# Macaron layer with two mixtures of experts: weights streamed past 128 stationary tokens in float32, each FFN in two turns of tokens

## The reference, cut to what matters

```python
# x: 16 batches x 256 tokens x 128; 8 experts, top 2, hidden 256; 16 heads of 4
x = x + 0.5 * ffn(layernorm(x), ...)
x = x + attention(layernorm(x), ...)          # softmax attention on the left 64 columns
x = x + 0.5 * ffn(layernorm(x), ...)          # the same weights again

def ffn(x, gate_w, gate_b, w0, b0, w1, b1, w2, b2):
    xt = x.reshape(-1, 128)                   # 4096 tokens
    logits = xt @ gate_w.T + gate_b           # 8 a token
    top_v, top_i = top_k(logits, 2)
    h0, h1 = xt @ w0[e].T + b0[e], xt @ w1[e].T + b1[e]     # 256 wide, for each expert e
    act = h0 * silu(h1)
    out = act @ w2[e].T + b2[e]               # 128 wide
    return softmax(top_v) . out[top_i]        # the two experts' rows, weighted
```

## Time and profile before

| | us |
|---|---|
| three runs | 880.24, 880.10, 875.22 |
| median | 880.1 |
| the profiled execution's own time | 880.13 |
| its span in the trace | 878.4 |
| mean granted TensorE clock | 0.876 of full speed |
| busy in the span: TensorE, VectorE, ScalarE, GpSimd | 539.3, 582.1, 393.3, 483.7 |

### The profile page before, as it was taken

The page is one execution under the profiler, slowest core; times in us unless marked ns, Lnnn a source line. Parts: engine busy times, 40 slices in busy tenths (PEclk is TensorE's granted clock), DMA queues, the critical chain, the costliest instruction groups (busy, mean ns, idle before and its releaser), DMA issues. The chain is left out here.

```text
span 878.4 us, 15667 instructions
## 1 busy us (share of the span) xinstructions
PE 539.3 (61%) x4422; PEld 406.5 (46%) x4422; DVE 582.1 (66%) x1878; ACT 393.3 (45%) x863; POOL 483.7 (55%) x584
## 2 busy tenths in 40 slices
PE   1222213999931468888877788778841296977830
PEld 1121213999930125555545455444420285867720
DVE  2346461888852677888878788878332196979928
ACT  1011012888820016666555555556620285757710
POOL 1367775566637974554656564422344256877850
PEclk9999999999975559999989899999975598998965
DMA  7211122333311211211112111110000222222226
GB/s 253 74 42 41 37 72 80 87 104 105 99 58 37 60 52 46 59 56 53 58 41 65 42 62 45 51 42 15 15 30 32 74 67 62 72 77 67 72 86 240
DMA packets 48705, 59.92 MB, mean 68 GB/s; under 512 B 10908, under 2 KB 40668, under 8 KB 47804
## 3 DMA queue, kind: packets, MB, share of 16 engines
q1 hardware_dynamic: 39420, 40.81, 15.2%
q0 software_dynamic: 8640, 17.84, 6.3%
q10 hardware_dynamic: 560, 0.27, 0.1%
HBM read 30.96 MB, written 27.44 MB: 66 GB/s over the span
## 5 line engine op out<-in xcount | busy, mean ns | idle before, releaser
L1074 DVE TENSOR_REDUCE attn_nm<-ps 128x2 f32<-128x512 f32 x256 | 170.1, 685 | 58.1 <-PE ps L777 41.7
L884 ACT ACTIVATE attn_pt<-ps 128x512 f32<-128x512 f32 x256 | 147.5, 597 | 105.7 <-PE ps L761 78.6
L299 POOL DMA_INDIRECT x_rows<-route_xn,route_rows x128 | 129.9, 1015 | 74.9 <-DVE route_rows L288 39.0
L777 PE MATMUL ps<-attn_ka,attn_qa 128*128 128x256 bf16 x512 | 109.7, 302 | 58.5 <-DVE attn_nm L1074 28.7
L761 PE MATMUL ps<-attn_qa,attn_ka 128*128 128x256 bf16 x512 | 103.0, 286 | 23.1 <-ACT attn_pt L884 12.2
L621 POOL DMA_INDIRECT y_tokens<-experts_y_tokens,experts_to x78 | 77.5, 993 | 54.1 <-DVE experts_y_tokens L540 35.9
L437 PE MATMUL ps<-experts_x_hi,experts_w 128*128 128x256 f32 x312 | 96.8, 310 | 7.0 <-issue 7.0
L438 PE MATMUL ps<-experts_x_lo,experts_w 128*128 128x256 f32 x312 | 89.9, 288 | 0.0
L439 PE MATMUL ps<-experts_x_hi,experts_w 128*128 128x256 f32 x312 | 89.9, 288 | 0.0
L777 PEld LDWEIGHTS ps<-attn_ka,attn_qa 128*128 128x128 bf16 x512 | 41.2, 103 | 94.7 <-DVE attn_nm L1074 48.2
L583 POOL CAST experts_w<-w_table 128x1536 fp32r x39 | 59.0, 1514 | 40.2 <-ACT experts_y L494 40.2
(11 more groups left out here) (178 smaller groups left out, 1286.3 us busy)
## 6 DMA issues: line engine op xcount, KB each, us to landing
experts_x<-x_rows SPq DMA_DIRECT2D x78, 130.0 KB
y_rows<-experts_y_tokens SPq DMA_DIRECT2D x39, 128.0 KB, 1.7
second_y<-y_tokens SPq DMA_DIRECT2D x16, 256.0 KB, 4.8
kq_pieces<-attn_kqp SPq DMA_DIRECT2D x16, 192.0 KB
x_rows<-no_rows SPq DMA_DIRECT2D x16, 130.0 KB
x_rows<-route_xn,route_rows POOLq DMA_INDIRECT x128
out<-x_tokens SPq DMA_DIRECT2D x16, 128.0 KB, 1.8
x_tokens<-x SPq DMA_DIRECT2D x7, 256.0 KB, 6.6
```

Source lines behind the costliest of these rows:

```text
L299: nc.gpsimd.indirect_dma_start(out=x_rows[:, :], out_offset=to, in_=xn[:, g % RX, t, :], in_offset=None).then_inc(sent[g % RX], 16)
L777: mm = pe.matmul(ps[:, SA[k], j * S:(j + 1) * S], qa[sl][:, h, qc * P:(qc + 1) * P], ka[sl][:, h, :], start=True, stop=True)
L884: nc.scalar.activation(pt[:, g % 2, j, :], ps[:, SBK[h % 2], :], ACT.Exp, scale=SCALE).then_inc(exp_done, 1)
L1074: nc.vector.tensor_reduce(nm[:, qc, 2 * pair:2 * pair + 2], ps[:, SA[k], :].rearrange("p (j t) -> p j t", t=S), AX.X, ALU.max, negate=True ...
```

## The change

- Each FFN has two turns of 2048 tokens (4 groups). A turn has its own list of at most 40 blocks of 128 slots, taken as 20 pairs; 40 pairs an FFN. There are two tensors `x_rows`, used in turn.
- In the first FFN only groups 0 to 3 are routed ahead of the blocks. Groups 4 to 7 are routed beside the 20 pairs of the first turn, at steps written out in TOP; their list is made at step 13. The list of the second FFN's first turn is made inside attention. The routing of the last group moves from the end of attention to the first steps of the second FFN's blocks, and the list of the last turn with it.
- The zeroing of `kq_pieces` moves behind the first loads of x; VectorE doesn't wait for it any more.
- The tokens are stationary and the weights move. `w_table` and `w2_table` hold plain float32; no split, no copies of weights. TensorE reads 10 experts at a time into registers and takes the weights at a register address. First layer: one float32 matmul of 512 columns for each half of the pair (w1 and w0 side by side). Second: two of 128 columns, after four transposes of the activation a pair.
- The biases are added by a bf16 matmul: `b_table` has each expert's biases as three bf16 pieces, on 24 partitions; `chosen` has, for each expert, ones on its three rows.
- For one pair ScalarE has silu and the copy of the transposed activation (512 elements each), VectorE the product (512), the copies of x and y (256 each), and in the second FFN three small operations in `dve_to`.
- SP reads 8 tail rows and 10 start rows at a time, and loads x by two DMAs a pair. A tail is 128 rows.
- In the second FFN, the y rows of the first 8 batches are loaded, added and stored beside the pairs of the last turn, from its fourth pair on.

```diff
+TURNS = 4
+TURN_GROUPS = 2 * GROUPS // TURNS
+SLOTS = 128
+PAIRS = -(-((2 * TURN_TOKENS + E * (SLOTS - 1)) // SLOTS) // 2)
+LISTED = 2 * PAIRS
...
+        w_table = sb("w_table", [P, E, WCOLS])
+        w2_table = sb("w2_table", [P, E, HID])
+        b_table, chosen = sb("b_table", [P, BCOLS], BF16), sb("chosen", [P, E, P], BF16)
...
+    def starts_of(eng, turn, blocks):
+
+        cols = listed[0:1, turn, 0, blocks.start:blocks.stop]
+        return nc.values_load_multi_w_load_instructions(cols, engines=(eng.engine,), min_val=0, max_val=ROWS - SLOTS)[1]
...
+    def streamed(table, e, at, n):
+        return table[:, bass.ds(e, 1), at:at + n].rearrange("p a w -> p (a w)")
...
+    def pe_first(pe, q):
+        pe.wait_ge(xT_done, q + 1)
+        wait(pe, act_done, q - 1)
+        if q % PAIRS % AT_ONCE == 0:
+            turn, js = some(q)
+            pe.wait_ge(route["list_ready"], 3 * (turn + 1))
+            for j, e in zip(js, route["experts_of"](pe, turn, js)):
+                expert[turn * LISTED + j] = e
+        for i in range(2):
+            e, o = expert[2 * q + i], ps[:, q % 2 * 2 + i, :]
+            pe.matmul(o, m["xT"][:, q % 2, i], streamed(w_table, e, W1, 2 * HID), start=True, stop=False)
+            mm = pe.matmul(o, streamed(chosen, e, 0, P), b_table[:, 0:2 * HID], start=False, stop=True)
+        mm.then_inc(h_ready, 1)
+
+    def pe_turn(pe, q):
+        pe.wait_ge(act_done, q + 1)
+        wait(pe, at_done, q)
+        for i in range(2):
             for k in range(CH):
...
+                mm = pe.transpose(ps[:, AT, (i * CH + k) * P:(i * CH + k + 1) * P], m["act"][:, q % 2, i, k * P:(k + 1) * P],
+                                  const["ident"][:])
+        mm.then_inc(aT_ready, 1)
+
+    def pe_second(pe, q):
+        pe.wait_ge(at_done, q + 1)
+        wait(pe, y_copied, q)
+        for i in range(2):
+            e, o = expert[2 * q + i], ps[:, Y, i * P:(i + 1) * P]
+            for k in range(CH):
+                pe.matmul(o, m["actT"][:, q % 2, i, k], streamed(w2_table, e, k * P, P), start=(k == 0), stop=False)
+            mm = pe.matmul(o, streamed(chosen, e, 0, P), b_table[:, 2 * HID:BCOLS], start=False, stop=True)
         mm.then_inc(y_ready, 1)
...
+    def pe(pe, q, own):
+        if q in own:
+            pe_first(pe, q)
+        if q + AHEAD in own:
+            pe_x(pe, q + AHEAD)
+        if q - TURN_LAG in own:
+            pe_turn(pe, q - TURN_LAG)
+        if q - Y_LAG in own:
+            pe_second(pe, q - Y_LAG)
...
+        for at in route["tails_of"](sp, turn):
+            sp.dma_start(x_rows[turn % 2][bass.ds(at, SLOTS), :], const["no_rows"][:, 0]).then_inc(tails, 16)
         sp.wait_ge(route["list_ready"], 3 * (turn + 1))
         route["all_sent"](sp, turn)
...
+    def sp_x(sp, q):
+        turn = q // PAIRS
+        if q % PAIRS == 0:
+            sp_list(sp, turn)
+        if q % PAIRS % AT_ONCE == 0:
+            _, js = some(q)
+            for j, at in zip(js, route["starts_of"](sp, turn, js)):
+                start[turn * LISTED + j] = at
...
+    TOP = {4: 1, 5: 4, 6: 8, 7: 11}
+    FIND = (2, 15)
+    LIST = TOP[7] + 2
...
-            dve.wait_ge(zeros_out, 16 * NB)
...
             route["dve_norm"](dve, 1)
-            for g in range(GROUPS):
+            for g in range(TURN_GROUPS):
...
+                if g == 0:
+                    dve.wait_ge(upto_done, 2)
+                    nc.vector.tensor_reduce(taken[:], const["piece"].rearrange("p (e i) -> p e i", i=PIECES), AX.X,
+                                            ALU.add).then_inc(chosen_made, 1)
+                    dve.wait_ge(chosen_made, 2)
+                    nc.vector.tensor_copy(chosen[:], taken[:].unsqueeze(2).broadcast_to([P, E, P])).then_inc(chosen_made, 1)
+                if g == 1:
+                    dve_biases(dve)
...
+            for q in all_steps:
+                blocks["sp"](sp, q, own)
+                if q == own.start:
+                    for b in range(NB):
...
+    HALF_OUT, TAKE = 4, 6
...
+                if q == middle + HALF_OUT:
+                    blocks["out_to"](sp, middle)
+                    sp_load(sp, range(NB // 2))
+                if 0 <= q - middle - TAKE - 1 < NB // 2:
+                    sp_store(sp, q - middle - TAKE - 1)
```

More of the change, by code:

```diff
@@ L190, in pe_transpose @@
         pe.wait_ge(xn_ready, g + 1)
-        wait(pe, prod_done, g - len(BANKS[g // GROUPS]) + 1)
+        for before in [i for i in range(g) if bank(i) == bank(g)][-1:]:
+            pe.wait_ge(prod_done, before + 1)
+            turn, at = divmod(before, TURN_GROUPS)
+            if at == TURN_GROUPS - 1:
+                pe.wait_ge(list_ready, 3 * turn + 1)
+                pe.wait_ge(list_step, LIST_STEPS * turn + 1)
         for t in range(TG):
@@ new lines, in y_offset, with experts_of @@
+    def y_offset(tile, r):
+        g, t = divmod(tile, TG)
+        return bass.IndirectOffsetOnAxis(ap=y_at[:, g, r, t:t + 1], axis=0)
+    def starts_of(eng, turn, blocks):
+        cols = listed[0:1, turn, 0, blocks.start:blocks.stop]
+        return nc.values_load_multi_w_load_instructions(cols, engines=(eng.engine,), min_val=0, max_val=ROWS - SLOTS)[1]
+    def experts_of(eng, turn, blocks):
+        cols = listed[0:1, turn, 1, blocks.start:blocks.stop]
+        return nc.values_load_multi_w_load_instructions(cols, engines=(eng.engine,), min_val=0, max_val=E - 1)[1]
@@ L374, in sem, with experts @@
+def experts(nc, c, route, const, tables, ps, x_rows, y_rows, y_tokens):
+    XR, YR, IR = 4, 4, 6
+    AT_ONCE = 5
+    XT, AT, Y = 4, 5, 6
+    AHEAD, TURN_LAG, Y_LAG = 2, 1, 2
+    ONE = PAIRS * (TURNS // 2)
+    w_table, w2_table, b_table, chosen = tables
     def sem(n):
@@ L402, in allocate @@
         sb("y_tokens", [P, YR, 2, P])
-        if turn:
+        if ffn:
+            sb("first", [P, 2, 2])
             sb("row", [P, 2, 2])
             m["to"] = late.enter_context(nc.sbuf_tensor("experts1_to", [P, IR, 2], U32))
-    def steps(turn, before, after):
-        own = range(turn * LISTED, (turn + 1) * LISTED)
-        return range(own.start - before, own.stop + after), own
-    def wait_out(eng, j):
-        first = len(range(j % YR, LISTED, YR))
-        uses = j // YR + 1
-        wait(eng, y_out[j % YR], 16 * min(uses, first))
-        wait(eng, y_sent[j % YR], 32 * (uses - first))
@@ L419, in pe_x, with steps, wait_out, some @@
-    def pe_x(pe, j):
-        pe.wait_ge(x_in[j % XR], 16 * (j // XR + 1))
-        wait(pe, xlo_done, j)
+    def steps(ffn):
+        own = range(ffn * ONE, (ffn + 1) * ONE)
+        return range(own.start - AHEAD, own.stop + Y_LAG + 1), own
+    def wait_out(eng, q):
+        first = len(range(q % YR, ONE, YR))
+        uses = q // YR + 1
+        wait(eng, y_out[q % YR], 16 * min(uses, first))
+        wait(eng, y_sent[q % YR], 32 * (uses - first))
+    def some(q):
+        turn, at = divmod(q, PAIRS)
+        return turn, range(2 * at, min(2 * (at + AT_ONCE), LISTED))
@@ new lines, in sp_y, with sp @@
+    def sp_y(sp, q):
+        sp.wait_ge(y_copied, q + 1)
+        sp.dma_start(y_rows[q * 2 * SLOTS:(q + 1) * 2 * SLOTS, :].rearrange("(i p) d -> p i d", i=2),
+                     m["y_tokens"][:, q % YR]).then_inc(y_out[q % YR], 16)
+    def sp(sp, q, own):
+        if q == own.start - AHEAD:
+            for i in range(XR):
+                sp_x(sp, own.start + i)
+        n = q + AHEAD + XR - 1
+        if n in own and n >= own.start + XR:
+            sp_x(sp, n)
+        if q - Y_LAG - 1 in own and q - Y_LAG - 1 < ONE:
+            sp_y(sp, q - Y_LAG - 1)
@@ L1571, in _ @@
+            blocks["out_to"](sp, own.stop)
+            sp_load(sp, range(NB // 2, NB))
+            for b in range(NB // 2, NB):
+                sp_store(sp, b)
             sp.wait_ge(stored, 16 * NB)
```

735 lines of the change are left out of this document (338 added, 397 removed).

## The result

The changed kernel takes 963.25 us (median of 4 runs, 961.48 to 965.88); the kernel before, run beside it, 880.17: ratio 1.096, interval 1.090 to 1.101. The forecast was 883 us, the range 850 to 928. The profiled execution has a span of 959.9 us at a mean clock of 0.872.

What follows compares the result with a forecast made beforehand. The prediction saw no single bound before, and TensorE's 3.9 us pairs bounding both FFNs' blocks after; +15.7 (first FFN), +1 (attention) and -13.5 (second FFN) gave +3.2 on 878.4, forecast 883 us, range 850 to 928.

Steps and rivals of the forecast that it cites:

- The pair: TensorE's work for two blocks of 128 slots: 3.9 us, with the other engines' work all under that.
- R3: Rival: on TensorE a float32 column costs one cycle an instruction, 68 us less, about 815 us; chance 0.07.
- The start: Routing of half the tokens ahead of the first FFN: first block at 91 us, where it was 147.06.
- I take 2 us hidden, 1.3 exposed: 7 batches after the first, 9.1 us an FFN: TensorE's register reading of ten experts every 5 pairs: 3.3 us a batch, partly covered by its queue.
- R1: Rival: TensorE's register batches exposed nearly in full, and addresses costing issue time: +41 us, 924 us; chance 0.26.
- half clock in the blocks: TensorE's clock at half in the FFN blocks, named among what would make all the theories wrong.
- The rest of the first FFN: First FFN's blocks besides the batches: pairs 156 us, routing 6.2, half-clock start 1.7, tables and waits 3, drain 1.2.
- The start of the second FFN: SP's chain from the last group's routing start to the first block: 21.5 us, where it was 46.4.
- The slack of 2 us at the second turn: First FFN: the second turn's x arrives at step 17.4, needed by step 18; each us beyond is on the path.
- R4: Rival: routing doesn't fit beside the first FFN's blocks, +22 us, 905 us; sign: gap at the 21st pair; chance 0.03.
- Attention's +1: Attention keeps its work and gains one list of blocks made inside it: 1 us longer.

Runs made afterwards that it cites:

- e7: e1's kernel with the first layer's operands rounded to float32r and multiplied in one instruction instead of two, less exact: 808.26 us, ratio 0.956.
- e10: e1's kernel run again, on the same chip as e9: 857.91 us, ratio 1.013.
- e6: Changed kernel with the eight tails of the second FFN's first turn written by SP at the end of attention: 908.84 us, ratio 1.072.
- e4: Changed kernel with the last turn's eight tails written by SP at its step 6 in the second FFN: 961.04 us, ratio 1.083.
- e5: Changed kernel with all of attention's block list but the two operations reading the counts moved two groups later: 913.34 us, ratio 1.078.
- e9: The changed kernel itself, run again on another chip: 914.17 us, ratio 1.080.
- e3: Changed kernel with the same batches of ten read one pair earlier, right behind the first layer's matmuls: 939.12 us, ratio 1.062.
- e2: Changed kernel with the batches of ten numbers that TensorE reads placed 64 bytes apart: 946.89 us, ratio 1.071.
- e1: Changed kernel with TensorE reading two experts ahead of each pair instead of ten ahead of every fifth: 916.37 us, ratio 1.035.
- e8: Changed kernel with the edits of e1, e4, e5 and e6, attention's last sends moved behind it, y loaded in twos: 838.51 us, ratio 0.990.
- e12: e8's edits with e7's one-pass float32r first layer, less exact there: 791.71 us, ratio 0.935.

## Why the prediction was wrong, by its own steps

| from the trace, us | forecast | measured |
|---|---|---|
| first block matmul | 91 | 86.1 |
| first FFN's blocks | 177.2 | 200.4 |
| attention, to the last update of x | 399.0 | 404.5 |
| to the second FFN's first block | 22.0 | 31.8 |
| its blocks | 171.7 | 214.5 |
| tail | 20.8 | 22.7 |
| span | 881.6 | 959.9 |

- **The pair was right**: 3.9 forecast, 3.92 measured, and one that needs nothing else on the way: no other engine's work is in it. That a float32 column costs two instructions of two cycles, read from attention's 379 against 277 ns, held (e7: half the instructions, 1.22 us less). R3 falls.
- **The start was right** to 5 us, on the early side: the last send before it began at 71.2 (73.5 forecast), and the eight tails took 4.0 us to issue where 11 were taken.
- **The step that failed is "I take 2 us hidden, 1.3 exposed: 7 batches after the first, 9.1 us an FFN".** The mechanism was named, and R1 was its full price, but the batch was mis-sized. The load: 1.5 taken, 1.1 or 2.5 measured, 1.84 in the middle. The arithmetic: 1.75 taken by its recorded length, 2.9 by its pitch. Hidden: 2 taken, 2.4 measured at the sixth reading, but 0.9 at the second, behind a few short matmuls of the routing. The gaps are 21.3 and 19.1 us where 9.1 each were forecast. The Trainium skill (Runtime: NRT & Kernel Launch, section Instruction fetch mechanics), as quoted with the sum, has about 200 ns a register, stated there for loads from HBM. By it ten registers would take 2.0 us, an estimate; the trace, whose numbers lie in SBUF, has 1.1 and 2.5.
- **What no step had is the clock behind the gaps.** The forecast gave 1.7 us an FFN to it, for a cold start, and named half clock in the blocks only as what would make all wrong. The windows have 0.96 and 0.89 of full clock in the blocks. With it, the reading costs 56 us (e10), where the forecast had 18 (14 x 1.3) and R1 51 (14 x 3.65). R1, with 0.26 of the chance and 924 us, comes closest, in part by luck: its 3.65 a batch is above the mean gap of 2.9, and the clock, which it did not have, makes up for that.
- **The rest of the first FFN was right.** Without readings the forecast for its blocks is 168.1 us (177.2 - 9.1); e10, which hides them, has 168.5 (82.86 to 251.32). For the second FFN it is 162.6 against 180.4, where x comes late twice in e10 (6.90 and 3.14).
- **The start of the second FFN missed 10 us**, the beginning of its code, for which VectorE waits 8.5 us. The forecast started SP at the statistics as if nothing stood between. The chain from SP's first reading, at 699.8, to the first block was 22.9 us where 21.5 were forecast, which is near by luck: the tails took 4.0 and not 8.5, and the readings, the landing and TensorE's own batch more than they were given. e6 takes 9.1 of it away.
- **The slack of 2 us at the second turn** was worked out for the first FFN alone, where it held: no gap at its 21st pair. In the second FFN x of a pair waits also for VectorE's places of the pair four before (`dve_to`), so SP starts its list one pair later: 6.98 us (e4). That is R4's sign, a gap at the 21st pair, but in the other FFN. The loads of y and the reading of ten starts behind them (869.7 to 877.1 in SP's queue) hold up x once more: 2.57.
- **Attention's +1** was 6.5. The list holds VectorE 3.4 us at a stretch (573.0 to 576.5 in the changed kernel), and by e5 a batch is 3.7 us longer for it. Why the rest, e5 doesn't say.

So of the 78 us missed, some 38 are the reading and its clock (56 less the 18 forecast), 10 the change of code, about 10 late x, 5 attention; the start is 5 better, the tail 2 worse. The remaining some 18 go with the 'remote' waits in the blocks, which end in a gap of 5.15 us on TensorE at 750.86, and their half clock: on e9's chip, almost without them, the change costs 66 us instead of 83. That last part is argued from two profiles, not shown by an experiment.

## What to carry to other kernels

A register reading on the bounding engine is priced by its pitch in the queue, not by the lengths of its rows; keep each one shorter than what the engine's queue covers (here two values each pair instead of ten each fifth), and, as e3 has it, put it behind the longest instructions. A gap on TensorE is paid twice when the clock falls behind it: sum the gaps, then look at the durations of the matmuls behind each. Streaming float32 at 4 cycles a column is paid for in full wherever TensorE is the bound: here 1.2 us of 3.9 a pair, which only the earlier start and shorter tail can earn back, and then by 1%.

## What the runs showed of the hardware

- A load of ten 4-byte values into TensorE's registers took 1.07 to 1.27 us for the first and third batch of a turn and 2.4 to 2.6 for the second and fourth, where the batches lie 40 bytes apart; on SP's queue, from the same tile, 0.95 to 1.3 and 2.1 to 2.4 in the same order. At a distance of 64 bytes all sixteen of TensorE took 1.07 to 1.4 (e2). Two values took 0.54 (e10), eight on SP's queue 0.53 to 0.75.
- The arithmetic and check of one value are recorded with 0.146 and 0.018 us but follow each other every 0.29 us on TensorE's queue.
- In the profiles of the result and of e1 to e4 ScalarE and VectorE stood for up to 9 us at a time on a releaser that the profile calls 'remote', in both kernels (41 us in all before, in attention; 77 after, 39 of them in attention); the profiles of e5 to e8 have none and those of e9 to e12 one each, of 1.6 us at most, and on these chips the kernel before took 847 and 848 us instead of 880. What it is, no run says.
- In the result's profile TensorE's clock was at its lower level behind readings with gaps of 3.09, 3.30, 3.37, 3.74 and 4.8 us in the blocks, and at its upper behind those of 1.69 to 2.16, but also behind 3.04 and 3.25. In e9 those two were followed by the lower level, and in e2 one of 2.25 was. The length of the gap alone doesn't decide it.
